# Four-layer graph network: layer-norm scale from ScalarE's root and VectorE's reciprocal, against a power on GpSimd with a Newton step on VectorE

## The reference, cut to what matters

```python
def _layernorm(x, axis=-1, eps=1e-5):
    m = jnp.mean(x, axis=axis, keepdims=True)
    v = jnp.var(x, axis=axis, keepdims=True)
    return (x - m) / jnp.sqrt(v + eps)

x = _layernorm(x + _L0_gnn_ref(x, adj, embedding, weight, bias))   # x, A x, A(A x), node-wise weights
x = _layernorm(x + _L1_gnn_ref(x, adj, a))                         # attention with a mask adj > 0.5
x = _layernorm(x + _L2_gnn_ref(x, adj, W, b))                      # (A + I) x W, over the degree
x = _layernorm(x + _L3_gnn_ref(x, adj, ..., 0))                    # three passes of A v and a small MLP
```

## Time and profile before

| | |
|---|---|
| median of 3 runs | 1052.36 us (1052.09 to 1052.92) |
| the profiled execution: its own time | 1052.66 us |
| its span | 1050.9 us |
| TensorE clock granted, mean | 0.996 of full |
| PE busy | 1023.4 us (97%), 6922 instructions |
| DVE busy | 690.4 us (66%), 1728 instructions |
| POOL busy | 538.1 us (51%), 625 instructions |
| ACT busy | 453.4 us (43%), 1097 instructions |
| DMA | 45.66 MB, nearly all in the first 75 us |

### The profile page before, as it was taken

The page is one execution under the profiler, slowest core; times in us unless marked ns, Lnnn a source line. Parts: engine busy times, 40 slices in busy tenths (PEclk is TensorE's granted clock), DMA queues, the critical chain, the costliest instruction groups (busy, mean ns, idle before and its releaser), DMA issues.

```text
span 1050.9 us, 18768 instructions
## 1 busy us (share of the span) xinstructions
PE 1023.4 (97%) x6922; PEld 490.9 (47%) x6922; DVE 690.4 (66%) x1728; ACT 453.4 (43%) x1097; POOL 538.1 (51%) x625
## 2 busy tenths in 40 slices
PE   7999999999999999999999999999999999999995
PEld 3445444434443444344345555555554545455553
DVE  3876565677547765775674778876546677767556
ACT  4632333333334343534423677557556622132632
POOL 0005486546456766775671757579764232223311
PEclk9999999999999999999999999999999999999998
DMA  9930000000000000000010121212112100000022
GB/s 365 400 128 1 2 1 2 1 2 1 1 1 2 1 1 2 1 1 2 1 41 1 41 81 41 81 41 80 53 69 81 41 1 1 3 2 21 22 61 61
DMA packets 14658, 45.66 MB, mean 43 GB/s; under 512 B 960, under 2 KB 9280, under 8 KB 10080
## 3 DMA queue, kind: packets, MB, share of 16 engines
q1 hardware_dynamic: 14560, 44.39, 11.4%
HBM read 40.19 MB, written 4.19 MB: 42 GB/s over the span
## 4 chain that ended last, share of the span: by engine, by line
PE 84%; DVE 9%; POOL 2%; ACT 2%; DMA 2%; issue 1%; SPq 0%; POOLq 0%; ACTq 0%; DVEq 0%
PE PS L750 34%; PE PS L880 21%; PE PS L924 18%; DMA BW<-at_in 2%; PE PS L735 2%; PE PS L737 2%; PE PS L736 2%; DVE BW L1200 1%; DVE T L1203 1%; DVE X L1203 1%; PE PS L744 1%; PE PS L742 1%; PE PS L743 1%; ACT T L1043 1%; PE PS L725 1%
## 5 line engine op out<-in xcount | busy, mean ns | idle before, releaser
L750 PE MATMUL PS<-BW,S 128*128 128x512 fp8e4 x1792 | 403.5, 379 | 4.3 <-POOL S L1708 1.9
L750 PEld LDWEIGHTS PS<-BW,S 128*128 128x128 f16 x1792 | 169.6, 98 | 211.0 <-issue 15.9
L1043 ACT ACTIVATE T<-PS,SM 128x128 f32<-128x128 f32 x384 | 112.5, 365 | 206.9 <-DVE X L1203 137.7
L880 PE MATMUL PS<-WZ,R 64*128 64x512 f16 x1536 | 198.5, 377 | 3.1 <-ACT T L1043 3.1
L1745 POOL TENSOR_TENSOR T<-T 128x128 f32<-128x128 f32 (+1 forms) x192 | 127.0, 662 | 124.9 <-ACT T L1043 114.4
L1203 DVE SCALAR_TENSOR_TENSOR X<-PS,SM,X 128x128 f32<-128x128 f32 x320 | 109.9, 344 | 38.7 <-PE PS L880 38.5
L880 PEld LDWEIGHTS PS<-WZ,R 64*128 64x128 f16 x1536 | 69.2, 94 | 106.8 <-issue 25.4
L924 PE MATMUL PS<-BW,S 128*128 128x512 fp8e4 x512 | 115.4, 379 | 0.4 <-issue 0.4
L1745 POOL TENSOR_TENSOR S<-R,S 128x512 f16<-128x512 f32 x48 | 57.5, 1210 | 94.2 <-ACT S L1043 94.2
L880 PE MATMUL PS<-WZ,T 64*128 64x512 f16 x768 | 103.8, 376 | 0.0
L1203 DVE SCALAR_TENSOR_TENSOR T<-PS,SM,T 128x128 f32<-128x128 f32 x256 | 88.0, 344 | 21.2 <-PE PS L880 21.2
(11 more groups left out here) (215 smaller groups left out, 1476.9 us busy)
## 6 DMA issues: line engine op xcount, KB each, us to landing
WZ<-a_in SPq DMA_DIRECT2D x16, 1024.0 KB, 4.8
BW<-at_in SPq DMA_DIRECT2D x8, 1024.0 KB, 18.3
R<-at_in SPq DMA_DIRECT2D x7, 1024.0 KB, 13.7
out<-X SPq DMA_DIRECT2D x16, 256.0 KB, 2.3
X<-x_in SPq DMA_DIRECT2D x3, 1024.0 KB, 20.3
T<-w_in SPq DMA_DIRECT2D x1, 1536.0 KB, 16.0
R<-at_in SPq DMA_DIRECT2D x2, 512.0 KB, 5.2
SM<-sm_in SPq DMA_DIRECT2D x1, 520.5 KB, 18.3
```

The lines of the kernel that those rows point to most:

```text
L750: m = e.matmul(o, stile(h, t, c), Bm[:, t, block(j)], start=(t == 0 and h == 0), stop=(last and t == NT - 1 and h == 1))
L880: m = e.matmul(bank(b0 + q), halves[kd][zh][r, :], WZ[r, wh, kd, block(g)], start=(i == 0), stop=(i == 8))
L1043: return e.activation(o, i, f, **kw)
```

## The change

The root of the weights' maximum and the 20 roots of the norms leave ACT. POOL takes their place with `ALU.pow`, with exponents from two columns that it fills at the start (`cHalf`: 0.5 and -0.5). In a norm, `var` moves whole to POOL: it adds the epsilon and raises to the power -0.5. `rs` on DVE becomes four instructions, the Newton step and the scaling in one. No step changes its place in the list, except that `root3` is gone.

```diff
-        on(h, ("var3", *u), ("root3", *u), ("rs3", *u), *outs(n, s))
+        on(h, ("var3", *u), ("rs3", *u), *outs(n, s))
@@ scalar_head @@
-                elif jt == 10:
-                    e.wait_ge(s_wsqr, 1)
-                    fn(col(cT3), col(cT3), ACT.Sqrt).then_inc(s_wroot, 1)
@@ scalar_steps @@
-                elif kind in ("var", "root3"):
-                    L, c, j = (*norm_key(step), 0)[:3]
-                    m = 2 if L == 3 else 1
-                    e.wait_ge(s_var, VARN[norm_key(step)] + 1)
-                    fn(st_part(L, c, j, 1, m), st_part(L, c, j, 2, m), ACT.Sqrt).then_inc(s_sd, 1)
@@ vector_head, weights(11) @@
-                    e.wait_ge(s_wroot, 1)
-                    vc(ts(e, col(cZ), col(cT3), 1e-30, 1.0 / 1024, ALU.max, ALU.mult))
+                    e.wait_ge(s_wsqr, 3)
+                    vc(ts(e, col(cZ), col(cT3), 1.0 / 1024, None, ALU.mult))
@@ vector_steps @@
-                    ts(e, st_part(L, c, 0, 2), st_part(L, c, 0, 0), a, b, ALU.mult, ALU.add).then_inc(s_var, 1)
...
-                    e.wait_ge(s_sd, VARN[norm_key(step)] + 1)
+                    e.wait_ge(s_pw, VARN[norm_key(step)] + 1)
...
-                    fc(e.reciprocal(s1, s1))
-                    fc(e.tensor_tensor(s0, s1, s1, ALU.mult))
-                    fc(e.tensor_tensor(s0, s0, s2, ALU.mult))
-                    fc(ts(e, s0, s0, -0.5, 1.5, ALU.mult, ALU.add))
-                    e.tensor_tensor(s2, s1, s0, ALU.mult).then_inc(s_rs, 1)
+                    m, eps = norm_scale(L)
+                    fc(e.tensor_tensor(s2, s1, s1, ALU.mult))
+                    fc(stt(e, s2, s0, eps, s2, ALU.add, ALU.mult))
+                    fc(ts(e, s2, s2, -0.5 * m ** 0.5, 1.5 * m ** 0.5, ALU.mult, ALU.add))
+                    e.tensor_tensor(s2, s1, s2, ALU.mult).then_inc(s_rs, 1)
@@ gpsimd_head @@
+            e.memset(col(cHalf), 0.5)
+            e.memset(col(cHalf + 1), -0.5)
...
             e.partition_all_reduce(col(cT3), wst[:, 0:1], 128, RED.max).then_inc(s_wsqr, 1)
+            e.wait_ge(s_wsqr, 1)
+            e.tensor_scalar(col(cT3), col(cT3), 1e-36, None, ALU.max).then_inc(s_wsqr, 1)
+            e.wait_ge(s_wsqr, 2)
+            e.tensor_tensor(col(cT3), col(cT3), col(cHalf), ALU.pow).then_inc(s_wsqr, 1)
@@ gpsimd_steps @@
+                elif kind in ("var", "var3"):
+                    L, c, j = (*norm_key(step), 0)[:3]
...
+                        e.wait_ge(s_red, REDN[L, c, 3] + 1)
+                    s0, s1 = (st_part(L, c, j, k, 2 if L == 3 else 1) for k in range(2))
+                    pc(e.tensor_scalar(s1, s0, norm_scale(L)[1], None, ALU.add))
+                    e.tensor_tensor(s1, s1, col(cHalf + 1).broadcast_to(list(s1.shape)), ALU.pow).then_inc(s_pw, 1)
```

More of the change, by code:

```diff
@@ L31 @@
 cSG, cISG, cKG = 36, 40, 44
+cHalf = 46
 cF = 50
@@ L228, in last_order @@
         u = ending(n, s, 0)
-        on(h, ("var3", *u), ("root3", *u), ("rs3", *u), *outs(n, s))
+        on(h, ("var3", *u), ("rs3", *u), *outs(n, s))
     r, (u, v), (x, y) = ending(7, 4, 0), [ending(7, 5, jj) for jj in range(2)], [ending(7, 6, jj) for jj in range(2)]
-    on(54, ("var3", *r), ("root3", *r), ("F", *u), ("sq", 3, *u), ("rs3", *r), *outs(7, 4))
+    on(54, ("var3", *r), ("F", *u), ("sq", 3, *u), ("rs3", *r), *outs(7, 4))
     on(55, ("F", *v))
     between[55] = [("F", *x), ("sq", 3, *v), ("var3", *u)]
-    on(56, ("root3", *u), ("rs3", *u), *outs(7, 5), ("F", *y), ("sq", 3, *x), ("sq", 3, *y), ("var3", *x), ("root3", *x),
+    on(56, ("rs3", *u), *outs(7, 5), ("F", *y), ("sq", 3, *x), ("sq", 3, *y), ("var3", *x),
        ("rs3", *x), *outs(7, 6))
@@ L329, in gnn_kernel @@
         s_xa = sem("s_xa")
-        s_wb, s_wsq, s_wsqr, s_wroot, s_wz, s_whi, s_wlo = (
-            sem(f"s_{k}") for k in ("wb", "wsq", "wsqr", "wroot", "wz", "whi", "wlo"))
+        s_wb, s_wsq, s_wsqr, s_wz, s_whi, s_wlo = (
+            sem(f"s_{k}") for k in ("wb", "wsq", "wsqr", "wz", "whi", "wlo"))
         s_p1, s_u1h, s_u1, s_nr, s_sign, s_q, s_dg = (
@@ L342, in gnn_kernel @@
         s_pc, s_fc = sem("s_pc"), sem("s_fc")
-        s_sq, s_red, s_var, s_sd, s_rs = (sem(f"s_{k}") for k in ("sq", "red", "var", "sd", "rs"))
+        s_sq, s_red, s_pw, s_rs = (sem(f"s_{k}") for k in ("sq", "red", "pw", "rs"))
         s_n = [sem(f"s_n{k}") for k in range(4)]
@@ L638, in number_norms @@
                     held[buf] = x[1:]
-                elif x[0] in ("var", "root3"):
+                elif x[0] in ("var", "var3"):
                     VARN[norm_key(x)] = len(VARN)
@@ L662, in sq_buf, with norm_scale @@
             return SQ[0] if L < 2 else SQC[2 * L - 4 + [y for y in SQN if y[0] == L].index((L, c, j)) % 2]
+        def norm_scale(L):
+            return ((64 * 4096, 1e-5 * 64), (64 * 4096, 1e-5 * 64 * 4096), (64 * 4096, 1e-5 * 64 * 4096), (64, 1e-5 * 64 * 4096))[L]
         def st_part(L, c, j, k, m=1):
@@ L1471, in vector_steps @@
                     red(e, o if L == 3 else o[:, 8 * j:8 * j + 8], grid(sq_buf(L, c, j)), ALU.add).then_inc(s_red, 1)
[L1472 to L1475, removed]
+                elif kind in ("rs", "rs3"):
+                    L, c, j = (*norm_key(step), 0)[:3]
+                    e.wait_ge(s_pw, VARN[norm_key(step)] + 1)
+                    if L == 3:
+                        r = order3(c, j) // 2
+                        e.wait_ge(*((s_n[1], 16) if r < 2 else (s_n[3], 2 * r - 2)))
+                    elif L < 2 and c >= 2:
                         e.wait_ge(s_n[L], 4 * (c - 1))
@@ L1478, in vector_steps @@
                         e.wait_ge(*((s_n[0], 12 + 4 * c) if c < 2 else (s_n[2], 4 * (c - 1))))
-                    a, b = ((1 / 64 / 4096, 1e-5 / 4096), (1 / 64 / 4096, 1e-5), (1 / 64 / 4096, 1e-5))[L]
-                    ts(e, st_part(L, c, 0, 2), st_part(L, c, 0, 0), a, b, ALU.mult, ALU.add).then_inc(s_var, 1)
[L1481 to L1492, removed]
-                    e.wait_ge(s_sd, VARN[norm_key(step)] + 1)
-                    s0, s1, s2 = (st_part(L, c, j, k, 2 if L == 3 else 1) for k in range(3))
-                    fc(e.reciprocal(s1, s1))
-                    fc(e.tensor_tensor(s0, s1, s1, ALU.mult))
-                    fc(e.tensor_tensor(s0, s0, s2, ALU.mult))
-                    fc(ts(e, s0, s0, -0.5, 1.5, ALU.mult, ALU.add))
-                    e.tensor_tensor(s2, s1, s0, ALU.mult).then_inc(s_rs, 1)
+                    s0, s1, s2 = (st_part(L, c, j, k, 2 if L == 3 else 1) for k in range(3))
+                    m, eps = norm_scale(L)
[3 more added lines that the diff above has]
+                    e.tensor_tensor(s2, s1, s2, ALU.mult).then_inc(s_rs, 1)
                 elif kind == "apply":
@@ L1783, in gpsimd_steps @@
                     e.wait_ge(s_add, n4 + 1)
+                elif kind in ("var", "var3"):
+                    L, c, j = (*norm_key(step), 0)[:3]
+                    if L == 3:
+                        for i in (j, j + 1):
+                            if summed_by_act(c, i):
+                                e.wait_ge(s_sq, SQN[3, c, i] + 1)
+                            else:
+                                e.wait_ge(s_red, REDN[3, c, i] + 1)
+                    else:
+                        e.wait_ge(s_red, REDN[L, c, 3] + 1)
+                    s0, s1 = (st_part(L, c, j, k, 2 if L == 3 else 1) for k in range(2))
+                    pc(e.tensor_scalar(s1, s0, norm_scale(L)[1], None, ALU.add))
+                    e.tensor_tensor(s1, s1, col(cHalf + 1).broadcast_to(list(s1.shape)), ALU.pow).then_inc(s_pw, 1)
                 elif kind == "sum":
```

## The result

The changed kernel takes 1104.4 us (median of 5; 1103.3 to 1106.7), the kernel before beside it 1052.8: a ratio of 1.0495, 95% interval 1.0482 to 1.0508, or 51.6 us slower. The forecast was 1058.4 with a range up to 1074. The direction was right and so were the head, layers 0 and 1 and the end as places; layer 2 was missed, and the size was far off.

What follows compares the result with a forecast made beforehand. PE, busy 97%, was taken as the bound, so other work counts only where PE or the end waits. Head +2.0, layer 1 +3.9 and last norm +0.2 sum to +6.1: 1058.8, as a median 1058.4 us; range 1053.2 to 1074.

Steps and rivals of the forecast that it cites:

- the head: Weights' scale at the start: POOL's pause after its configuration change makes `cZ` 2.0 us late, with nothing covering it, +2.0.
- the end: Last norm, from the last reduction to the scaled output: the power on POOL makes it longer, +0.2 us.
- The price of a power: POOL's power in each norm: 1.3 us for 128x32, between 0.28 (as an addition) and 6.9 us; 0.75 for 128x16.
- the upper end's case: A power on 128x32 that takes 6.9 us, the longest that anything holds POOL; it gives 1091 us.
- layer 1: Layer 1's norms: late ACT copies make PE wait 1.3 us at each of three chunks, +3.9 us.
- Layer 0: Layer 0's norms: about 1.5 us of room for a power of 1.3 us, so no cost.
- Layer 2 at nothing: Layer 2's norms: PE has no wait on ACT or DVE nearby, so they cost zero.
- ScalarE's table loads and roots at nothing: Eight table loads outside the head, 10.3 us of ACT, and the head's root: removing them gains zero.
- the rival "faster": ACT's relief reaches PE, whose 3.1 us of waits on ACT go, with a cheap power: 1048.9 us, chance 0.05.
- the rival of a cheap power: A power on POOL costs as little as an addition, 0.28 us for 128x32: +2.4, 1054.8 us, chance 0.17.
- The rival of the slow power: A power on POOL takes 6.9 us for 128x32, so the norms' latency costs +39: 1091 us, chance 0.12.

Runs made afterwards that it cites:

- layer 2 alone: The kernel before, with only layer 2's four norms done as in the change: 1062.3 us, ratio 1.0092.
- The head alone: The kernel before, with only the head's root done as in the change: 1055.6 us, ratio 1.0024.
- the kernel with layer 0 alone: The kernel before, with only layer 0's four norms done as in the change: 1065.4 us, ratio 1.0124.
- the kernel with half a power: The kernel before, with only layer 1's norms as in the change and their power on 16 of the 32 columns: 1068.6 us, ratio 1.0155.

## Why the prediction was wrong, point by point

**The price of a power: mis-sized, and it is most of the miss.** The step took "the middle in ratio", 1.3 us for 128x32, between an addition and the longest hold of POOL (that middle is 1.39). It measured 5.45, near the upper end. For a step that multiplies into seven places, a middle in ratio over a factor 25 was no price; the range should have reached to the upper end's case. With 5.45 in the prediction's own sums: layer 1 is 2.4 + 4.15 - 1.1 = 5.45 us a norm, and 5.50, 5.50 and 5.07 were measured. Layer 0 is 5.45 - 1.5 - 1.1 = 2.85, three times 8.6; measured 9.2, though spread unevenly. The end is 0.2 + 2.2 = 2.4, measured 3.4: from the last reduction to the output it is 2.65 us longer (4.31 in place of 1.66), and the reduction itself comes 0.77 later behind PE's last matmuls, DVE having idled 0.94 us for the norm before the last. The head would be 2.3. All together 30, or 1082 us: the mechanism held at these places, and the prediction's sums still fall 22 us short.

**The lowered clock: a term that the sum did not have.** 11.6 us in the profiled execution. The trace before had no such stretch behind its short waits (the longest on layer 1's path is 0.9 us). It showed only that the clock falls once PE has stopped: behind the last matmul, from 1042.3 us on, the granted clock is 0.52. So it could not be priced, but a forecast of waits of several microseconds on PE should have left room for it.

**Layer 2 at nothing: wrong.** The step said that the norms of layer 2 "stand where PE has no wait on ACT or DVE nearby". That is about PE; the row to read was POOL's queue, in which the norm now stands behind layer 1's splits. In the change that is 7.1 us of waiting; alone, layer 2 costs 9.6 us, 5.6 of it waiting and 3.0 the clock. The run with the norm moved ahead confirms the queue for the first of the two places. For the other, near 765 us in the change, no run was made, and the trace of layer 2 alone shows only 1.2 us of queue there; why DVE is so late by then stays open.

**The head: right, with some luck.** POOL was forecast to start at 44.90 and started at 44.93, ACT's half at "near 46.0" and came at 46.48. That POOL's start agrees is luck: the pause was 7.76 us, not 6.93, but the maximum came 0.8 earlier. The power on one column was 0.60, not 0.22. The head alone costs 2.9 us (1.6 to 3.5 by its interval) where 2.0 was forecast.

The Trainium skill ("GPSIMD Engine Reference", § 2.1 Instruction dispatch) gives 5.95 us for the first call to freshly loaded code. The trace agrees that there is such a pause, and not on its length: 7.76 us here, and the measured pause decides.

**ScalarE's table loads and roots at nothing: right**, for the table loads by the run that removes them alone (ratio 1.0000). The rival "faster" is refuted with it and by the changed kernel's own time, and the rival of a cheap power by the group of 5448 ns. That rival's time of 1054.8 came out 2.4 low: 1057.15 with the power left out. The rival of the slow power was the nearest to what came, at a chance of 0.12, and its 1091 us were too low too, although it took 6.9 us for a power that takes 5.45: it had neither the clock nor layer 2 in it.

## What to carry to other kernels

An operation that no row shows, put on a path at many places, is not priced by a middle value: let the range and the chances run over both ends, or ask what the sum is if the dear end holds. When work moves to an engine that is "half idle", read that engine's queue at every place where it lands, for what stands ahead of it and what it now stands ahead of. And where one engine sets the time, relief of another is worth at most what it waits there for, which was 3.1 us here, and the relief turned out to bring none of it.

## What the runs showed that I had not expected

- A two-operand power on GpSimd takes 0.157 us for each element of a partition, some 75 times an addition (2.1 ns by the earlier trace rows): 5.45 us for 32, 2.95 for 16, 1.68 for 8, 0.60 for one. The exponent one is no cheaper (5.42 us) than -0.5.
- Waits of PE of some 3.3 us were followed by 1.6 us of loss to the lower clock, waits of 5.6 by 2.6, and waits of 11 by 2.7. But the length of a wait does not set it. The same three waits of layer 1 (5.5, 5.5 and 5.1 us) cost 5.3 us in the change and 7.7 alone. Waits of 1.55 and 3.17 us in the kernel with layer 0 alone were followed by no lowered clock, yet the same place in the change, where the wait is 3.19, was (0.29 us for a 128x128 matmul at once, 0.22 in the other). What PE had waited shortly before doesn't tell it either: the first wait of 3.27 us in the kernel with half a power had nothing above 1.1 us in the 100 us ahead of it, and the clock fell all the same. What does set it stays open.
- DVE's instructions on 128x32 took 1.0 us in layer 2 while POOL worked through its fp8 additions, where the same took 0.2 to 0.4 otherwise, before the change as after it.
